# An attention and mixture-of-experts layer: all nine down products as plain fp32 products

## The reference

```python
scores = jax.nn.sigmoid((xf @ gate_w.T).astype(jnp.float32))
_, sel = jax.lax.top_k(scores + expert_bias[None, :], TOP_K)      # 8 experts, 2 are taken
...
h = jax.nn.silu(routed @ w1[e].T) * (routed @ w3[e].T)            # routed = token x score
out_r = out_r + jnp.where(m, h @ w2[e].T, ...)                    # then times the score again
shared = jax.nn.silu(xf @ sw1.T) * (xf @ sw3.T) @ sw2.T           # a ninth expert for all tokens
```

## Time and profile before

| | |
|---|---|
| time, median of 3 runs | 840.73 us (838.68 to 842.02) |
| the profiled execution | 841.74 us |
| its span, first to last instruction | 839.9 us |
| busy over the span: PE, DVE, ACT, POOL | 762.2, 711.9, 556.9, 528.4 us |
| expert stage on TensorE | 464.60 us to the end |
| granted TensorE clock, mean | 0.981 |

### The profile page before, as it was taken

The page is one execution under the profiler, slowest core; times in us unless marked ns, Lnnn a source line. Parts: engine busy times, 40 slices in busy tenths (PEclk is TensorE's granted clock), DMA queues, the critical chain, the costliest instruction groups (busy, mean ns, idle before and its releaser), DMA issues.

```text
span 839.9 us, 19474 instructions
## 1 busy us (share of the span) xinstructions
PE 762.2 (91%) x6228; PEld 472.2 (56%) x6228; DVE 711.9 (85%) x1430; ACT 556.9 (66%) x1128; POOL 528.4 (63%) x686
## 2 busy tenths in 40 slices
PE   2688999999999999999996989999999999999994
PEld 1234555555555555555544666666666666666662
DVE  5587999999999999999982788788888788887885
ACT  1148888888888888888882556555555555565651
POOL 3447766676676677667324466667666766666664
PEclk9999999999999999999998799999999999999997
DMA  5644656557556566655314524334443444445420
GB/s 157 170 114 131 172 162 176 159 145 188 148 157 175 153 171 154 177 162 141 97 34 124 129 81 113 97 108 99 112 117 115 119 125 125 125 125 119 120 86 27
DMA packets 201682, 109.36 MB, mean 130 GB/s; under 512 B 10496, under 2 KB 201088, under 8 KB 201600
## 3 DMA queue, kind: packets, MB, share of 16 engines
q1 hardware_dynamic: 200048, 105.88, 46.7%
q10 hardware_dynamic: 1552, 2.44, 1.0%
HBM read 73.94 MB, written 33.82 MB: 128 GB/s over the span
## 4 chain that ended last, share of the span: by engine, by line
PE 58%; issue 12%; POOL 10%; DVE 9%; DMA 6%; ACT 3%; SPq 1%; DVEq 1%; POOLq 0%; ACTq 0%
PE bank L724 14%; PE bank L696 10%; PE bank L709 7%; POOL place L510 4%; DMA probs<-route_dram 4%; PE bank L731 4%; DVE k_stack L1075 3%; PE bank L732 3%; PE bank L733 3%; PE bank L889 3%; PE bank L806 2%; POOL rstd L519 2%; PE bank L786 2%; PE bank L826 2%; PE bank L793 2%
## 5 line engine op out<-in xcount | busy, mean ns | idle before, releaser
L1001 DVE TENSOR_REDUCE negmax<-bank 128x2 f32<-128x512 f32 x512 | 320.3, 679 | 26.5 <-PE bank L709 23.9
L558 ACT ACTIVATE probs<-bank 128x512 f32<-128x512 f32 x512 | 291.7, 605 | 60.9 <-PE bank L696 57.3
L709 PE MATMUL bank<-k_stack,q_stack 48*128 48x256 bf16 x1024 | 163.4, 283 | 9.7 <-DMA k_stack<-k_parts_dram 5.6
L696 PE MATMUL bank<-q_stack,k_stack 50*128 50x256 bf16 x1024 | 156.6, 274 | 4.0 <-ACT probs L558 3.5
L731 PE MATMUL bank<-x_hi,hi_w 128*128 128x512 f32 x288 | 138.4, 481 | 11.1 <-DVE k_stack L1075 8.1
L724 PE MATMUL bank<-probs,v_aug 128*32 128x256 f32 x2048 | 137.9, 387 | 0.4 <-ACT attT L569 0.4
L1065 DVE TENSOR_TENSOR k_stack<-bank,probs 128x512 f32<-128x512 f32 x128 | 87.6, 684 | 45.6 <-DMA probs<-route_dram 27.2
L696 PEld LDWEIGHTS bank<-q_stack,k_stack 50*128 50x128 bf16 x1024 | 75.4, 95 | 87.7 <-ACT probs L558 44.4
L732 PE MATMUL bank<-x_hi,lo_w 128*128 128x512 f32 x288 | 115.8, 402 | 0.0
L733 PE MATMUL bank<-x_lo,hi_w 128*128 128x512 f32 x288 | 115.6, 401 | 0.0
L510 POOL TENSOR_TENSOR k_stack<-k_stack,probs 128x512 f32<-128x512 f32 x48 | 62.1, 1294 | 80.5 <-DVE k_stack L1075 72.0
(11 more groups left out here) (113 smaller groups left out, 1326.8 us busy)
## 6 DMA issues: line engine op xcount, KB each, us to landing
probs<-route_dram SPq DMA_DIRECT2D x128, 256.0 KB, 5.9
q_stack<-q_parts_dram SPq DMA_DIRECT2D x64, 192.0 KB, 3.3
k_stack<-k_parts_dram SPq DMA_DIRECT2D x64, 192.0 KB, 4.0
k_parts_dram<-k_parts SPq DMA_DIRECT2D x32, 192.0 KB, 2.2
q_parts_dram<-q_parts SPq DMA_DIRECT2D x32, 192.0 KB, 2.1
xT_sb<-xT SPq DMA_DIRECT2D x32, 128.0 KB, 2.2
k_parts_dram<-k_parts SPq DMA_DIRECT2D x32, 128.0 KB, 2.0
q_parts_dram<-q_parts SPq DMA_DIRECT2D x32, 128.0 KB, 2.0
```

What stands on the lines that cost most here:

```text
L558: nc.scalar.activation(probs[h][:], score_ps[EXP_BANK[h]][:].rearrange("p (j t) -> p j t", j=NT), ACT.Exp).then_inc(exp_done, 1)
L696: mm = pe.matmul(score_ps[EXP_BANK[h]][:, j * T:(j + 1) * T], k_stack[b.ring][first:last, h // 2, j * P:(j + 1) * P], q_stack[b.ring][firs ...
L709: mm = pe.matmul(max_ps[MAX_BANK[h]][:, i * T:(i + 1) * T], q_stack[b.ring][first:last, h // 2, i * P:(i + 1) * P], k_stack[b.ring][first: ...
L1001: nc.vector.tensor_reduce(negmax[b.ring % 2][:, :, column], max_ps[MAX_BANK[h]][:].rearrange("p (i s) -> p i s", i=NT), AX_X, ALU.max, neg ...
```

## The change

All nine down products of a group become plain fp32 products of unsplit w2 and unsplit `hid_s` (`hid` for product 0), three buffers deep as before. The high and low parts of these inputs are no longer made: ScalarE loses five copies a group, VectorE three subtractions, GpSimd two. The high and low parts of w2 go as well, and w2 is loaded once, at the start, into a buffer of its own with all nine experts. `hid_s` of every product may now be overwritten only when its down product has been formed. No other instruction changes its place.

```diff
-        w_hi, w_lo = ([sb(f"{part}_{n}", [P, NE, P], F32R) for n in ("w1", "w3", "w2")] for part in ("hi", "lo"))
+        w_hi, w_lo = ([sb(f"{part}_{n}", [P, NE, P], F32R) for n in ("w1", "w3")] for part in ("hi", "lo"))
+        w2_sb = sb("w2_sb", [P, NE, P])
...
-        def wait_used(engine, g, n):
-
-            if n % NE in WHOLE:
-                engine.wait_ge(down_mm, done(g, n))
-            else:
-                engine.wait_ge(hs_hi_set, split_done(g, n))
-                wait_lo(engine, g, n)
...
-                        for m in range(3):
+                        for m in range(2):
                             pool.wait_ge(w_hi_set, m + 1)
                             pool.tensor_tensor(w_lo[m][:], w_stage[m], w_hi[m][:], ALU.subtract).then_inc(w_lo_set, 1)
...
                         if past(g, 1) or n > DEPTH:
 
-                            wait_used(pool, g, n - DEPTH)
+                            pool.wait_ge(down_mm, done(g, n - DEPTH))
                         pool.wait_ge(hid_set, done(g, n))
                         pool.wait_ge(square_set, g * E + n)
                         pool.tensor_tensor(hid_s[n % DEPTH], hid[n % DEPTH], weight2_b[n - 1],
                                            ALU.mult).then_inc(hids_set, 1)
-                    m = behind(g, n, POOL_LAG)
-                    if m is not None and m % NE in POOL_LO:
-                        low_part(g, m)
...
-                if not t.soft.looped and t.soft.c == B + 1:
-                    act_e.wait_ge(av_mm, 4 * B)
-                    act_e.dma_start(w2_whole, w2T[:, 0:w2_whole.shape[1]]).then_inc(w2_in, 16)
...
-                    m = behind(g, n, HI_LAG)
-                    if m is not None and m % NE in SPLIT:
-                        high_part(g, m)
...
-            pe.wait_ge(w2_in, 16)
...
-                wait_lo(pe, g, n)
+                if n % NE:
+                    pe.wait_ge(hids_set, routed(g, n))
+                else:
+                    pe.wait_ge(hid_set, done(g, n))
                 n %= NE
-                product(down_ps[r], 2, n, hs_hi[n % DEPTH], hs_lo[n % DEPTH], start=(n == 0), stop=(n == NE - 1)).then_inc(down_mm, 1)
+                pe.matmul(down_ps[r][:], w2_sb[:, n, :], (hid_s if n else hid)[n % DEPTH], start=(n == 0), stop=(n == NE - 1)).then_inc(down_mm, 1)
...
             def delayed(g, n):
-                m = behind(g, n, LO_LAG)
-                if m is not None and m % NE in DVE_LO:
-                    low_part(g, m)
                 m = behind(g, n, HID_LAG)
                 if m is not None:
                     hidden(g, m)
```

More of the change, by code:

```diff
@@ L192, in attention_moe_layer @@
         DEPTH = 3
-        LAG, HID_LAG, LO_LAG, HI_LAG, POOL_LAG = 4, 1, 3, 1, 1
+        LAG, HID_LAG = 4, 1
         places = [stack[:].rearrange("p h t -> p (h t)").bitcast(F32)[:, n * G:(n + 1) * G]
@@ L210, in attention_moe_layer @@
         x1_sb = [v.rearrange("p (a c) -> p a c", c=P) for v in take(2)]
-        w2_whole = v_aug[0][:].rearrange("p j u g c -> p (j u g c)").rearrange("p (n c) -> p n c", c=P)
         x_hi, x_lo = ([sb(f"x_{part}{r}", [P, G], F32R) for r in range(2)] for part in ("hi", "lo"))
-        hs_hi, hs_lo = ([sb(f"hs_{part}{r}", [P, G], F32R) for r in range(DEPTH)] for part in ("hi", "lo"))
-        w_stage = [x1T[:, m * NE * P:(m + 1) * NE * P].rearrange("p (n c) -> p n c", n=NE) for m in range(3)]
+        w_stage = [x1T[:, m * NE * P:(m + 1) * NE * P].rearrange("p (n c) -> p n c", n=NE) for m in range(2)]
         best = sb("best", [P, TILES])
@@ L222, in attention_moe_layer @@
         weight_in, x1_in = [sem(f"weight_in{e}") for e in range(E)], [sem(f"x1_in{r}") for r in range(2)]
-        w2_in, w_hi_set, w_lo_set, x_hi_set, x_lo_set = (sem(n) for n in ("w2_in", "w_hi_set", "w_lo_set", "x_hi_set", "x_lo_set"))
+        w_hi_set, w_lo_set, x_hi_set, x_lo_set = (sem(n) for n in ("w_hi_set", "w_lo_set", "x_hi_set", "x_lo_set"))
         gated_set, up_mm, act_set, hid_set, square_set, hids_set, down_mm = (
             sem(n) for n in ("gated_set", "up_mm", "act_set", "hid_set", "square_set", "hids_set", "down_mm"))
-        hs_hi_set, hs_lo_dve, hs_lo_pool = sem("hs_hi_set"), sem("hs_lo_dve"), sem("hs_lo_pool")
         outT_set, out_T, res2_set, stats2_set, mv2_set, eps2_set, rstd2_set, y_set, y_out = (
@@ L278, in routed @@
             return g * E + (n if n >= 0 else n + 1)
[L280 to L285, removed]
         def past(g, n):
@@ L494, in _ @@
             slots(pool, slot)
[L496 to L500, removed]
             def group(g, r):
@@ L521, in _ @@
             groups(pool, group)
-            for n in range(POOL_LAG):
-                if (n - POOL_LAG) % NE in POOL_LO:
-                    low_part(GROUPS, n - POOL_LAG)
             pool.wait_ge(eps2_set, GROUPS)
@@ L646, in square @@
                 nc.scalar.activation(weight2_b[e], weight_b[e], ACT.Square).then_inc(square_set, 1)
[L648 to L655, removed]
             act_e.wait_ge(x1T_kept, B)
@@ L679, in _ @@
             groups(act_e, group)
-            for n in range(HI_LAG):
-                if (n - HI_LAG) % NE in SPLIT:
-                    high_part(GROUPS, n - HI_LAG)
             drain(GROUPS, 1)
@@ L754, in slot @@
                 if not t.soft.looped and t.soft.c == B + 1:
-                    pe.wait_ge(w_lo_set, 3)
+                    pe.wait_ge(w_lo_set, 2)
                     pe.wait_ge(exp_done, H * B)
@@ L1071, in hidden @@
                 if n == DEPTH:
-                    wait_used(dve, g, 0)
+                    dve.wait_ge(down_mm, done(g, 0))
                 elif n > DEPTH or past(g, 1):
@@ L1075, in hidden @@
                 nc.vector.tensor_tensor(hid[n % DEPTH], up3_ps[n % DEPTH][:], act[n % DEPTH], ALU.mult).then_inc(hid_set, 1)
[L1077 to L1082, removed]
             def stats_of(g, r):
@@ L1145, in _ @@
             groups(dve, group)
-            for n in range(LO_LAG):
+            for n in range(HID_LAG):
                 delayed(GROUPS, n)
```

2 lines of the change are left out of this document (1 added, 1 removed).

## The result

The changed kernel takes 804.88 us (median; 803.53 to 806.83), the kernel before 839.7 us beside it: ratio 0.959, 95% interval 0.9547 to 0.9633. Two later comparisons gave 0.9564 (0.9536 to 0.9592) and 0.9555 (0.9521 to 0.959). The gain was forecast as 28 us and is 35. Of all runs behind this document one, of the kernel with the added wait alone, took 905.17 us at a granted clock of 0.801 where its nine others took 836.6 to 842.1, and it is left out of the comparisons.

The account below looks back on a forecast made before the run. A ring through four engines was taken to set 22.69 us a group, with TensorE the next bound. 841.74 - 22.9 - 0.5 - 4 = 814.3, with the profiled execution 1.0 above the median: 813 us, range 805 to 826.

Parts of the forecast that it names:

- the added wait: GpSimd's hid_s(n) also waits for down(n-3) where that was split; hid_s(8) may start at 2.6 us, earlier than before.
- four stretches of the table: Forecast gains: start to the expert stage 0, groups 0 and 1 0.5, 13 steady groups 22.9, tail 4 us.
- rival E: All idle goes and attention gains a little, with 1 to 3 us in setup and start: 808 to 810 us; chance 0.10.
- The ring: Expert stage: norm, output write, routing-weight DMA, weighing, hid, power, next norm set the group; 22.68 us becomes 20.3.
- The idle that stays: TensorE's remaining idle in a steady group: bounded by 0 and 1.1 us, taken as 0.15.
- the spot at hid 6: Expert stage, weighing to hid 6: reached at 20.6 us, wanted at 20.78; the place with no room, decided by var_eps.
- the steady part: Expert stage, 13 groups going from 22.69 to 20.93 us each: -22.9 us.
- The four stops: TensorE's four waits a group, about 0.26 us restart each: two for hs_lo vanish, two hang on the ring.
- Start and tail: Groups 0 and 1: -0.5 us; kernel end, waits for the last down and ahead of hid 7: about -4, bounds -2 and -5.
- Setup: One low and one high part of weights go near 64 us; attention paced by VectorE and ScalarE: 0, bounds 0 and -1.

Follow-up runs that it names:

- the ring alone: Changed kernel with each down product cut to one stand-in pass behind the same waits: 785.68 us (one run), 19.60 us a group.

## Why the prediction was right, and where its sizes were off

**The number** was close to a miss. All four stretches of the table were forecast too small, by 2.2, 1.2, 2.2 and 2.1 us, which is 7.7 together, and the lower end of the range just took that up. What happened is nearer to rival E, all idle gone and attention a little faster, which had a chance of 0.10; its 808 to 810 us were too long by the ends.

**The ring** was the step that carried the forecast, and it is shown: 22.76 us a group with a quarter of TensorE's work taken out, 21.15 without VectorE's low part of product 5 (forecast 22.69 - 1.48 = 21.21, a fit with some luck, as told there), 21.80 without GpSimd's of product 8 (forecast 22.69 - 0.90 = 21.79). TensorE's 20.78 came out as 20.76.

**The idle that stays** was taken as 0.15 us a group and is 0. Two shares of the ring had been read as fixed lengths and were contention: var_eps (0.73 on average, 0.17 after) and the power step (1.46, 1.01 after). The durations fall by 1.0 us together. By the table 0.37 of it shortens the ring between var_eps and hid 6 and 0.28 behind hid 7, where GpSimd's three hid_s in a row take part of it back. 20.3 - 0.65 is 19.65, and the ring alone measured 19.6; so the spot at hid 6 that seemed to have no room has some. The 1.48 us of the low part were no fixed length either: some 0.9 of it was time held by GpSimd. The power step's 0.45 came from the low part of product 7, which VectorE had begun ahead of it: in the kernel before each power step but the last ends 0.86 or 0.87 us behind the end of that low part. So four of the five low parts were on the ring, two of them (3 and 7) by contention that the prediction didn't name; product 7 was not run alone. With 20.76 instead of 20.93 a group this is the 2.2 us of the steady part.

**The four stops.** Their explanation held: two vanished, two were the ring's. The runs with products 3 and 8 plain say it more sharply than the prediction did: the largest wait of the fullest engine was worth 0.37 us a group where 0.75 + 0.26 - 0.16 = 0.85 was to be expected from the wait list, and a subtraction that nobody waited for was worth 0.89.

**The added wait** is seen on GpSimd (0.85 us in the rows) and costs TensorE nothing.

**Start and tail** were mis-sized, 0.5 for 1.7 and 4 for 6.1 us. At the start the prediction counted the two stops for hs_lo (1.0 us); the stop for a hid product, which also fell, from 2.1 to 0.9 us, was not in its sum. In the tail only the waits for the last down and for hid 7 were counted; the downs of products 3, 5 and 7 waited for low parts there too, 0.91, 0.87 and 1.96 us, the last two with no up product left to stand in. And the clock differed. The last down and the last transposes of the kernel after, which answer to the earlier trace rows:

```profile
795.11 1.12 PE L829 MATMUL bank<-place,w_sb 128*128 128x512 f32 x2
796.92 0.66 PE L835 MATMUL bank<-ident,place 128*128 128x128 f32 x4 [0.69 <-ACT place L596]
```

The transposes took 1.11 us before. There the granted clock was 1.00 (2.4 GHz) up to 829 us, 0.59 on average in the next microsecond and 0.50 (1.2 GHz) from 830 us on, and TensorE had stood still for 1.96 us ahead of the down of product 7 and for 1.14 ahead of that of product 8. In the kernel after the clock is 1.00 until the transposes are done, and falls between 799 and 800 us.

**Setup** was taken as 0 with a bound of 1 us; 1.05 is what one wait in the traces shows for it. The reason given, that VectorE's and ScalarE's steady work paces attention, doesn't fit the trace of before: from 100 to 440 us TensorE is busy for 336.8 of the 340 us, VectorE for 329.7 and ScalarE for 292.0. The remaining 1.2 us of the first row of the table stay open.

## What to carry to other kernels

Follow the waits of the fullest engine back until they close on themselves: if a chain norm, DMA, weighing, power, norm has the length of the period, only what stands in that chain is worth removing, and the longest wait on the list may be worth less than half of what it shows. Then look at what runs beside each link: a short VectorE instruction may end right behind a GpSimd one every time, and then its length in the row is a wait that a change on GpSimd can take away. When the ring gets shorter than the work of the fullest engine, the next step is the reverse, to give cheap passes back to that engine and put their helpers where others wait.

## What the runs showed that was not expected

- VectorE and GpSimd hold each other. A 128 x 4 `tensor_scalar` on VectorE takes 0.17 us alone and up to 1.19 when it starts inside a GpSimd product; a 128 x 128 one 0.34 against 1.21 to 1.32. GpSimd's power step on 128 x 4 takes 1.01 us, and 1.46 when VectorE's low part (two SBUF inputs) was begun ahead of it. When it is the power step that began first, as with product 5 plain, neither is held: 1.01 and 0.70 us.
- Nine plain fp32 products in a group cost as much each as the four did before: 0.857 us in a stream, the time of 3.67 of this case's fp32r passes of 0.2335. That is a price in time; how many passes TensorE makes for it no row shows.
- One and the same kernel reaches the first power step of attention 82.7 to 86.4 us into the span: small gains ahead of that can't be read from single profiles.
